# Dot attention's last steps on GpSimd, tile by tile, within the slot loop of a graph network kernel

## What is computed

```python
def _L2_gnn_ref(embeds, qW, kW, vW, rows, cols):
    ...
    scores = jnp.clip(jnp.einsum('ehd,ehd->eh', q, k), -10.0, 10.0)
    exp_s = jnp.exp(scores)
    norms = jax.ops.segment_sum(exp_s, rows, num_segments=nvar)[rows]
    w = exp_s / (norms + 1e-08)
    res = jax.ops.segment_sum(w[:, :, None] * v, rows, num_segments=nvar).reshape(nvar, d)
    return embeds + res
...
h = jnp.maximum(_layernorm(x, axis=-1), 0.0)
x = x + _L2_gnn_ref(h, L2_gnn_qW, L2_gnn_kW, L2_gnn_vW, src, dst)
h = jnp.maximum(_layernorm(x, axis=-1), 0.0)
x = x + _L3_gnn_ref(h, edge_index, L3_gnn_W, L3_gnn_b)
```

## Time and profile before

| | |
|---|---|
| runs, us | 1628.04, 1626.44, 1622.48 (median 1626.44) |
| profiled execution, us | 1627.73, its span 1625.9 |
| busy in the span | PE 76%, DVE 77%, ACT 34%, POOL 23% |
| mean granted clock of TensorE | 0.885 |
| slot loop of the dot attention | about 1249.5 to 1526.4 us of the span |
| VectorE's L1980 to L1983 | 1530.87 to 1537.4 us |
| mean aggregation's first matmul | 1557.44 us |

### The profile page before, as it was taken

How to read it: one execution, slowest core, us unless ns; L and a number is a source line. 1 busy time by engine, 2 the same in 40 slices (tenths; PEclk the granted TensorE clock), 3 DMA queues, 4 the chain that set the end, 5 groups by cost and what they waited for, 6 DMA issues and landing times. The chain is left out here.

```text
span 1625.9 us, 44876 instructions
## 1 busy us (share of the span) xinstructions
PE 1237.4 (76%) x18543; PEld 1174.0 (72%) x18544; DVE 1259.8 (77%) x2302; ACT 546.2 (34%) x1096; POOL 373.9 (23%) x211
## 2 busy tenths in 40 slices
PE   4767777399999999999994004888856888888468
PEld 3356767399899999999993004787755887888368
DVE  7888888766566565665667998999988999999733
ACT  0047777400000000000002873333335777777311
POOL 1400000000000000000001012888862665656300
PEclk6858777699999999999997556999997999999789
DMA  0012222375475565654563683555513444543293
GB/s 10 0 46 109 105 103 109 109 249 190 151 240 204 161 196 194 213 194 164 203 213 110 225 298 123 204 201 189 200 68 117 144 159 149 164 146 122 96 343 101
DMA packets 74936, 256.85 MB, mean 158 GB/s; under 512 B 17999, under 2 KB 19576, under 8 KB 74732
## 3 DMA queue, kind: packets, MB, share of 16 engines
q1 hardware_dynamic: 59996, 211.70, 38.6%
q10 hardware_dynamic: 14400, 40.97, 6.5%
q0 software_dynamic: 336, 1.20, 0.3%
HBM read 168.15 MB, written 85.68 MB: 156 GB/s over the span
## 5 line engine op out<-in xcount | busy, mean ns | idle before, releaser
L1248 PE MATMUL psum<-work,count 128*128 128x192 f16 x6250 | 521.4, 247 | 30.7 <-issue 30.7
L1248 PEld LDWEIGHTS psum<-work,count 128*128 128x128 f16 x6250 | 519.7, 98 | 32.5 <-issue 31.8
L1171 DVE SCALAR_TENSOR_TENSOR work<-psum,small,work 128x96 f32<-128x96 f32 x250 | 79.5, 318 | 177.4 <-PE psum L1248 177.3
L1585 PE MATMUL psum<-count 128*128 128x98 f16 x625 | 113.1, 209 | 134.5 <-DVE count L1632 98.2
L1852 PE MATMUL psum<-count 128*128 128x100 f16 (+1 forms) x1875 | 181.4, 207 | 44.5 <-DVE count L1941 30.7
L1852 PEld LDWEIGHTS psum<-count 128*128 128x128 f16 x1875 | 162.7, 98 | 55.3 <-issue 36.0
L929 ACT ACTIVATE work<-work 128x1248 f32<-128x1248 f32 (+1 forms) x6 | 7.2, 1203 | 576.9 <-DVE work L912 576.8
L1917 POOL TENSOR_TENSOR count<-count 128x1000 bf16<-128x1000 f32 (+1 forms) x75 | 160.8, 2143 | 122.0 <-ACT count L1901 122.0
L1624 POOL TENSOR_TENSOR count<-count 128x970 bf16<-128x970 f32 (+1 forms) x75 | 166.7, 2236 | 91.2 <-ACT count L1617 91.2
L1853 PE MATMUL psum<-count 128*128 128x100 f16 (+1 forms) x1875 | 180.8, 207 | 0.0
L1853 PEld LDWEIGHTS psum<-count 128*128 128x128 f16 x1875 | 164.4, 98 | 0.0
(11 more groups left out here) (286 smaller groups left out, 2695.7 us busy)
## 6 DMA issues: line engine op xcount, KB each, us to landing
x<-bucket_rows_by_src SPq DMA_DIRECT2D x100, 400.0 KB, 4.6
onehots_by_src<-x ACTq DMA_DIRECT2D x100, 400.0 KB, 4.3
count<-bucket_rows_by_dst SPq DMA_DIRECT2D x50, 800.0 KB, 4.4
count<-onehots_by_src SPq DMA_DIRECT2D x50, 800.0 KB, 4.3
count_f<-count SPq DMA_DIRECT2D x25, 800.0 KB, 6.8
count<-count_turned SPq DMA_DIRECT2D x25, 800.0 KB, 5.8
count<-count_f SPq DMA_DIRECT2D x17, 800.0 KB, 4.3
count_turned<-x SPq DMA_DIRECT2D x25, 416.0 KB, 2.4
```

The costliest lines, as they stand in the source:

```text
L1248: last = nc.tensor.matmul(bank[i % BANKS], count16[:, j, i * P:(i + 1) * P], y[par][:, j, :], start=(j == 0), stop=(j == TILES - 1))
L1585: nc.tensor.matmul(ps[:, at:at + GW], node_hot[SRC][t % 2][:, s, :], high[:, s, :], start=True, stop=False, skip_group_check=True)
```

## The change

GpSimd divides and adds the node tiles 0 to 21 one at a time; VectorE keeps tiles 22 to 24. VectorE makes the reciprocals of tiles 0 to 10, 11 to 17 and 18 to 21 (`EARLY`) inside the slot loop, in slots 12, 19 and 23, right after `add` of slot 10, 17 and 21 (`invert`). GpSimd does one product (`scale_tile`) or one sum (`finish_tile`) behind each low part from group 38 on, up to group 72, and the four tiles 18 to 21 after the low part of the last group. The sum waits for the product by a semaphore. In the other branch (`many`) the work is done at the start of the last layer's block (`set_up`). The sums and products are the same as before.

```diff
--- before.py
+++ after.py
@@ -1740,12 +1740,31 @@
     result = region.take(TILES * VW).rearrange("p (t n) -> p t n", n=VW)
     inv = region.take(TILES * HEADS).rearrange("p (t h) -> p t h", h=HEADS)
     part = sq.rearrange("p t d -> p (t d)")
+    by_head = result.rearrange("p t (h j) -> p t h j", j=VH)
+    EARLY = ((0, 11), (11, 18), (18, 22))
+    LAST_EARLY = EARLY[-1][1]
+    finished = nc.alloc_semaphore("dot_tile_finished")
+
+    def scale_tile(pool, u):
+        nc.gpsimd.tensor_tensor(part[:, u * D:(u + 1) * D].rearrange("p (h j) -> p h j", j=DH), by_head[:, u, :, 0:DH],
+                                inv[:, u, :].unsqueeze(2).broadcast_to([P, HEADS, DH]), ALU.mult).then_inc(finished, 1)
+
+    def finish_tile(pool, u):
+        pool.wait_ge(finished, 2 * u + 1)
+        nc.gpsimd.tensor_tensor(x[:, u, :], x[:, u, :], part[:, u * D:(u + 1) * D], ALU.add).then_inc(finished, 1)
+
+    def finish_early_tiles(pool):
+        def many():
+            for u in range(LAST_EARLY):
+                scale_tile(pool, u)
+                finish_tile(pool, u)
+        if_one(pool, m, None, many)
     loaded, zeroed = nc.alloc_semaphore("dot_weights_loaded"), nc.alloc_semaphore("dot_weights_zeroed")
     projected, split, high_ready = (nc.alloc_semaphore("dot_" + k) for k in ("projected", "split", "high_ready"))
     RING = 8
     names = ["hot_%d%d" % (v, p) for v in range(2) for p in range(3)]
     S = {k: nc.alloc_semaphore("dot_" + k) for k in names + [
-        "cols", "q_done", "q_copied", "k_done", "multiplied", "reduced", "capped", "clipped", "v_done"]}
+        "cols", "q_done", "q_copied", "k_done", "multiplied", "reduced", "capped", "clipped", "v_done", "inverted"]}
     S.update(m["slots_done"])
     nodes = Turned(nc, m, h, hT, "dot")
 
@@ -1911,10 +1930,34 @@
 
             @block.gpsimd
             def _(pool):
-                for i, (s, t0, n) in enumerate(groups):
+                def lows(i):
+                    n = groups[i][2]
                     pool.wait_ge(S["high_done"], i + 1)
                     after(pool, S["scattered"], i - 2)
                     nc.gpsimd.tensor_tensor(value_low[i % 3][:, 0:n * VW], value[i % 2][:, 0:n * VW], value_high[i % 3][:, 0:n * VW], ALU.subtract).then_inc(S["low_done"], 1)
+
+                def one():
+                    for i in range(G):
+                        lows(i)
+                        for k, (u0, u1) in enumerate(EARLY[0:2]):
+                            step = i - ((u1 + 1) * PER + 2)
+                            u = u0 + step // 2
+                            if step >= 0 and u < u1:
+                                if step == 0:
+                                    pool.wait_ge(S["inverted"], 2 * k + 2)
+                                if step % 2 == 0:
+                                    scale_tile(pool, u)
+                                else:
+                                    finish_tile(pool, u)
+                    pool.wait_ge(S["inverted"], 2 * len(EARLY))
+                    for u in range(*EARLY[2]):
+                        scale_tile(pool, u)
+                        finish_tile(pool, u)
+
+                def many():
+                    for i in range(G):
+                        lows(i)
+                if_one(pool, m, one, many)
 
             @block.vector
             def _(dve):
@@ -1926,6 +1969,12 @@
                     nc.vector.tensor_tensor(edge_hot[s % 3].rearrange("p t (n d) -> p t n d", d=2),
                                             iota16.rearrange("p (n d) -> p n d", d=2).unsqueeze(1).broadcast_to([P, TILES, P // 2, 2]),
                                             cols[:, :, SRC, s, :].unsqueeze(2).broadcast_to([P, TILES, P // 2, 2]), ALU.is_equal).then_inc(S["edge_hot"], 1)
+
+                def invert(k, u0, u1):
+                    dve.wait_ge(S["added"], u1)
+                    nc.vector.tensor_scalar(inv[:, u0:u1, :].unsqueeze(3), by_head[:, u0:u1, :, DH:VH], 1e-8 * 2.0 ** -SCALE, None, ALU.add).then_inc(S["inverted"], 1)
+                    dve.wait_ge(S["inverted"], 2 * k + 1)
+                    nc.vector.reciprocal(inv[:, u0:u1, :], inv[:, u0:u1, :]).then_inc(S["inverted"], 1)
 
                 def add(s):
                     dve.wait_ge(S["scattered"], (s + 1) * PER)
@@ -1957,6 +2006,9 @@
                                 spot_edges(s + 1)
                         if t0 == GROUP and s >= 2:
                             add(s - 2)
+                            for k, (u0, u1) in enumerate(EARLY):
+                                if u1 == s - 1:
+                                    invert(k, u0, u1)
                 add(TILES - 2)
                 add(TILES - 1)
         end_round(nc, [*S.values(), *m["spots"].all()])
@@ -1975,17 +2027,19 @@
         def link(ins):
             dve.wait_ge(step.sem, step.up(ins))
 
-        by_head = result.rearrange("p t (h j) -> p (t h) j", j=VH)
-        inv_all = inv.rearrange("p t h -> p (t h)")
-        link(nc.vector.tensor_scalar(inv_all.unsqueeze(2), by_head[:, :, DH:VH], 1e-8 * 2.0 ** -SCALE, None, ALU.add))
-        link(nc.vector.reciprocal(inv_all, inv_all))
-        link(nc.vector.tensor_tensor(part.rearrange("p (i j) -> p i j", j=DH), by_head[:, :, 0:DH], inv_all.unsqueeze(2).broadcast_to([P, TILES * HEADS, DH]), ALU.mult))
-        link(nc.vector.tensor_tensor(m["x"], m["x"], part, ALU.add))
-
-    return last_loads_landed, vector_end
-
-
-def mean_aggregate(nc, m, ins, cnt_dram, turned_dram, out, dot_landed, dot_vector_end):
+        late = slice(LAST_EARLY, TILES)
+        inv_late = inv[:, late, :]
+        link(nc.vector.tensor_scalar(inv_late.unsqueeze(3), by_head[:, late, :, DH:VH], 1e-8 * 2.0 ** -SCALE, None, ALU.add))
+        link(nc.vector.reciprocal(inv_late, inv_late))
+        of_late = part[:, LAST_EARLY * D:TILES * D]
+        link(nc.vector.tensor_tensor(of_late.rearrange("p (t h j) -> p t h j", h=HEADS, j=DH), by_head[:, late, :, 0:DH], inv_late.unsqueeze(3).broadcast_to([P, TILES - LAST_EARLY, HEADS, DH]), ALU.mult))
+        link(nc.vector.tensor_tensor(x[:, late, :].rearrange("p t d -> p (t d)"), x[:, late, :].rearrange("p t d -> p (t d)"), of_late, ALU.add))
+        dve.wait_ge(finished, 2 * LAST_EARLY)
+
+    return last_loads_landed, vector_end, finish_early_tiles
+
+
+def mean_aggregate(nc, m, ins, cnt_dram, turned_dram, out, dot_landed, dot_vector_end, finish_dot_tiles):
 
 
 
@@ -2040,6 +2094,7 @@
             nc.scalar.copy(parts[:, t0:t1, 0:D], h[:, t0:t1, :]).then_inc(high, 1)
 
     def set_up(pool):
+        finish_dot_tiles(pool)
         nc.gpsimd.memset(parts[:, :, D:A], 1.0)
         nc.gpsimd.memset(parts[:, :, A + D:2 * A], 0.0)
 
```

## The result

The changed kernel took 1637.45 us (median of 8 runs) against 1627.24 us before: the ratio is 1.0055, with a 95% interval of 1.0034 to 1.0077. It is slower by about 9 us by the ratio, where I had forecast 1630.2 us, 3.8 more, in a range that ended at 1636, and had called that no measurable difference. One of the eight runs took 3768.8 us and is not in the ratio; nothing here explains it, and the median of the other seven is 1634.94 us. So whether the time lies in the range hangs on that one run; that the kernel is slower, and by more than the 0.23% forecast, does not.

A forecast was written before the change was run, and what follows sets the result against it. VectorE was taken to set the slot loop's pace, one slot every 10.82 us. Terms -5.14 (tail) + 1.97 (inversions) + 4.86 (hold) + 2.1 (GpSimd's end) = +3.8 us, giving 1630.2 us against the median 1626.44; range 1623 to 1636.

The forecast's parts named there:

- The price of a late VectorE: Slot loop: VectorE sets the pace, so whatever is put into its stream is paid in full, the others waiting.
- the next block: Block after the loop: VectorE's chain gets 5.1 us shorter against the loads, first matmul needs only the first load; cost 0.
- The tail: VectorE after the loop: the remaining work takes 1.40 us instead of 6.54, saving 5.14.
- The inversions' own price and the hold: VectorE in the loop: three inversions cost 1.97 us; GpSimd's low part stalls each tensor_scalar 1.62 us, 4.86 in all.
- The doubt about the stride: Inversions' tensor_scalar reads every 25 columns; traced stalls were of dense ones, so the stall could be 0 instead of 4.86 us.
- the pace of L1980: Strided tensor_scalar after the loop needed 127 ns for 75 columns, no gain of speed; by this the stall could be zero.
- I take 4.86: Slot loop: three tensor_scalars stand still until GpSimd's instruction ends, 1.62 us each, the upper bound of 0 to 4.86.
- all on the path: Slot loop: the three inversions' own 1.97 us on VectorE count in full, as all engines queue behind.
- GpSimd in the loop: 36 small GpSimd instructions of 0.36 us from group 38 on, hidden in gaps of at least 0.90 us; cost 0.
- GpSimd after the last low part: Loop's end: eight instructions for four tiles take 3.7 us, so the barrier waits 2.1 us for GpSimd.
- The rival of long GpSimd instructions: GpSimd's small instructions cost 0.87 us each, so 6.3 us of wait at the loop's end; +8.0, 1634.4 us; chance 0.17.

The follow-up runs named there:

- the plain delays: Kernel before plus one tensor_reduce on VectorE in slots 12, 19 and 23: loop 289.71 us (long) and 283.31 (short), against 276.58.
- the one with its chain cut: Kernel before without product L1982 and sum L1983, so the attention's result is not added: 374.59 us from the slot loop on, against 376.06.

## Why the prediction was wrong

Two steps failed. The price of a late VectorE was taken as one us of the loop for each us of delay, with nothing for TensorE's clock; each us of delay cost 1.5 to 1.7 us. And the next block was put at "cost 0"; the start of the mean aggregation alone cost 1.6 us, and the rest after it was 0.9 longer. Part by part:

*The tail*: right, -5.08 against -5.14.

*The inversions' own price and the hold*: right in kind, a little too large. The three tensor_scalars took 1.67, 1.65 and 1.64 us, so each was held for 1.47 us beyond the 0.20, 0.18 and 0.17 that they take free; I had 1.62. That sum counted the instruction's own time twice: L910 of the earlier trace rows ended 0.04 us after the memset, so its own time lies within the hold, and by that row the extra would have been 1.62 + 0.04 - 0.21 = 1.45. VectorE was late by 2.17, 2.05 and 1.96 us, 6.2 in all, where the terms gave 6.8. The doubt about the stride is settled: the strided one is held as the dense ones of the earlier trace rows are, and free of it once moved to where GpSimd is idle (0.20). The rule of the Trainium skill ("VectorE: DVE Perf Modes", section "Mode 2×_2P — use both read ports for one tensor", which names no condition on strides, and "SBUF — State Buffer", section "Who interferes with whom") was the better guide here than the pace of L1980, and the 1.67 us beside a GpSimd instruction agree with it.

*What failed is the sentence "I take 4.86"*, as the whole price of the hold, and with it "all on the path" at one us for each us of VectorE. A delayed VectorE costs more than its delay where TensorE's clock falls behind it, as it did behind each of the three: the slots cost 3.46, 3.07 and 3.40 us, which is 1.29, 1.02 and 1.44 beyond the delays, 3.75 in all, and the plain delays show the same without a hold. The sum had no term for TensorE, which was busy 116.97 of 137 us. That leaves slack only at the full clock. The 3.75, less the 0.65 by which the delays were overrated, and 0.16 at the two ends of the loop make the difference of 3.3 between 10.09 and 6.8.

*GpSimd in the loop*: right. Its instructions took 0.35 and 0.39 us against 0.36 and fitted in the gaps. (The line through L1917's two prices gives 889 ns for L191, not 883; nothing hangs on it.)

*GpSimd after the last low part*: right, 1.69 against 2.1. The wait of a sum for its product was about 0.08 us instead of 0.25.

*The next block, "cost 0"*: wrong. I saw that the chain got 5.1 us shorter against the loads, asked only whether the matmul's data would be there, and left out what else needs the DMA engines. Loads that were through at the block's end before were still under way at it, and the start came back when fewer were issued ahead. It cost 1.61 us at the start and 0.90 in the rest, together about half of the win in the tail; for the 0.90 the loads as the cause are not shown.

The two misses, 3.3 and 2.5 us, less 0.4 at the join, make the 5.4 between 3.8 and 9.2. The rival of long GpSimd instructions came closest to the measured time, but by luck: its mechanism did not occur. No rival named either of the two causes.

## What to carry to other kernels

Before a small instruction is put into VectorE's stream where VectorE sets the pace, look at what GpSimd is doing at that very moment: one group later the same three inversions cost 0.2 us instead of 10.1. Price a delay of the pacing engine by what it does to TensorE's clock too, and try it with a dummy instruction in the kernel before. And when a chain ahead of a barrier gets shorter, ask which transfers were through at the barrier and no longer are.

## What was not expected of the hardware

A delay of 1.16 us on VectorE cost 2.67 us where the granted clock fell and 1.15 where it did not, after nearly the same pause of TensorE. A reciprocal of 44 columns was not held by a GpSimd instruction that read SBUF (0.43 us beside it), while a tensor_scalar of the same size at the same place was (1.67 us). And transfers of 0.8 MB each, eight of them issued in a block and some still under way at its end, put off TensorE's first matmul in the next block by 1.6 us in the changed kernel and 2.1 in the one with its chain cut, though the first load had taken only 4.2 us to land in the former (issued at 1542.1, the matmul at 1562.14).
